# Sixteen-head attentions: the mask of the first pass moved from TensorE into VectorE's maximum

## The reference, cut to what matters

```
rel = k_off[None, :] - bs - q_off[:, None]
mask = (jnp.abs(rel) <= w) & valid            # w = bs = 128
scores = jnp.where(mask, q @ k.T * scale, -inf)
out = softmax(scores) @ v                     # then @ Wo.T (+ bo), added to x
```

## Time and profile before

| | |
|---|---|
| median of 3 runs | 3557.51 us (3554.87 to 3571.56) |
| the profiled execution: its own time | 3537.08 us |
| its span, from first to last instruction | 3535.1 us |
| TensorE matmuls busy | 2807.6 us (79%), 22894 instructions |
| VectorE busy | 1827.2 us (52%), 3518 instructions |
| ScalarE busy | 1385.0 us (39%) |
| GpSimd busy | 757.2 us (21%) |
| mean granted TensorE clock | 0.877 of full |
| units of the causal attention | 1268 to 1549 us of the span: 281.0 us |
| units of the sliding attention | 3199 to 3424 us of the span: 225.0 us |

### The profile page before, as it was taken

The page is one execution under the profiler, slowest core; times in us unless marked ns, Lnnn a source line. Parts: engine busy times, 40 slices in busy tenths (PEclk is TensorE's granted clock), DMA queues, the critical chain, the costliest instruction groups (busy, mean ns, idle before and its releaser), DMA issues. The chain is left out here.

```text
span 3535.1 us, 58022 instructions
## 1 busy us (share of the span) xinstructions
PE 2807.6 (79%) x22894; PEld 1440.1 (41%) x22894; DVE 1827.2 (52%) x3518; ACT 1385.0 (39%) x2680; POOL 757.2 (21%) x701
## 2 busy tenths in 40 slices
PE   6566877778887768889768888898887878777986
PEld 3455246523347533334322222342233433564545
DVE  5311244379874278811378888312773543626733
ACT  4210434442323337653356777422222222234551
POOL 1000006336516320000443340003530000230003
PEclk9675878978888879999979999998999989887987
DMA  2022001111101231000041010000520001022102
GB/s 110 15 64 75 0 13 40 44 61 66 66 13 41 76 69 32 22 1 0 14 71 22 11 31 1 0 0 17 132 64 0 0 1 48 17 54 66 40 5 70
DMA packets 85552, 130.19 MB, mean 37 GB/s; under 512 B 15584, under 2 KB 54464, under 8 KB 84008
## 3 DMA queue, kind: packets, MB, share of 16 engines
q1 hardware_dynamic: 73256, 108.26, 11.2%
q0 software_dynamic: 8576, 15.14, 1.8%
q10 hardware_dynamic: 3456, 3.15, 0.3%
HBM read 99.93 MB, written 25.85 MB: 36 GB/s over the span
## 5 line engine op out<-in xcount | busy, mean ns | idle before, releaser
L1758 DVE TENSOR_REDUCE at_mp<-PS 128x1 f32<-128x384 f32 (+3 forms) x640 | 306.4, 535 | 93.7 <-PE PS L1583 81.6
L1708 ACT ACTIVATE at_pt<-PS 128x384 f32<-128x384 f32 (+3 forms) x704 | 270.7, 455 | 198.5 <-PE PS L1583 165.0
L1575 PE MATMUL PS<-at_kx,at_qx 48*128 48x384 bf16 (+5 forms) x640 | 199.9, 349 | 67.5 <-PEq L77 41.0
L1603 PE MATMUL PS<-at_qx,at_kx 57*128 57x512 bf16 (+5 forms) x704 | 193.9, 315 | 9.7 <-ACT at_pt L1708 9.4
L4206 ACT ACTIVATE ls_pt<-PS,ls_far 128x512 f32<-128x512 f32 x256 | 155.3, 684 | 22.0 <-PE PS L4027 16.8
L4353 DVE CUSTOM_DVE_ANT_0 PS<-PS,ls_pt 128x1024 f32<-128x1024 f32 x128 | 153.7, 1239 | 17.8 <-ACT ls_pt L4206 15.2
L1583 PE MATMUL PS<-at_above,identb 64*128 64x128 bf16 (+1 forms) x1408 | 161.1, 212 | 0.0
L1583 PE MATMUL PS<-at_other,at_eye 64*128 64x128 bf16 (+1 forms) x1408 | 158.5, 208 | 0.0
L2478 DVE TENSOR_TENSOR_SCAN mb_ring<-PS,mb_ring 128x1024 f32<-128x1024 f32 x64 | 146.6, 2290 | 19.4 <-POOL mb_ring L2417 6.7
L2433 PE MATMUL PS<-mb_ring,ident 128*128 128x512 f32 x256 | 147.8, 730 | 6.0 <-DVE mb_ring L2483 6.0
L989 ACT ACTIVATE mx_h<-PS,small_L 128x128 f32<-128x128 f32 x312 | 88.9, 368 | 146.0 <-PE PS L873 79.2
(11 more groups left out here) (830 smaller groups left out, 6473.5 us busy)
## 6 DMA issues: line engine op xcount, KB each, us to landing
rw_arena<-rw_v_rows SPq DMA_DIRECT2D x32, 512.0 KB, 4.6
dl_arena<-in_fir_bank SPq DMA_DIRECT2D x32, 256.0 KB, 3.2
lnA<-mb_rows SPq DMA_DIRECT2D x16, 512.0 KB, 3.7
XN<-mb_rows SPq DMA_DIRECT2D x16, 512.0 KB, 3.6
ffn_place<-in_ffn_L SPq DMA_DIRECT2D x4, 1152.0 KB, 17.0
x_rows<-mx_t SPq DMA_DIRECT2D x16, 256.0 KB, 2.4
mx_s<-y_rows SPq DMA_DIRECT2D x16, 256.0 KB, 5.0
ffn_place<-in_ffn_L SPq DMA_DIRECT2D x4, 1024.0 KB, 7.9
```

Source lines behind the costliest of these rows:

```text
L1575: mm = nc.tensor.matmul(PS[:, n % 3, 0:e - c], QX[rows, u % 3, g, blk(i, P)], KX[rows, u % 3, g, c:e], start=True, stop=True)
L1603: mm = nc.tensor.matmul(PS[:, 3 + n % 3, 0:e - c], KX[rows, u % 3, g, blk(j, P)], QX[rows, u % 3, g, c:e], start=True, stop=True)
L1708: nc.scalar.activation(PT[:, y % SLOTS, g, 0:e - c], PS[:, 3 + n % 3, 0:e - c], ACT.Exp, scale=SCALE).then_inc(exp_done, 1)
L1758: nc.vector.tensor_reduce(best, sc, AX.X, ALU.max).then_inc(s_maxed, 1)
```

## The change

A table `HIDE` (128 x 512, fp32) holds +1e30 at the places that the mask hides and 0 elsewhere: in its last block for the causal attention, in its first and third for the sliding one. Where a piece of the first pass has a cut block, VectorE's instruction is `tensor_tensor_reduce` instead of `tensor_reduce`: it subtracts the fitting stretch of `HIDE` from the scores in PSUM, writes the difference back to PSUM in place, and gives the maximum. Pieces without a cut block keep `tensor_reduce`. `score_masks` goes, and the score's matmul signals `s_ready` itself. The second pass and its masks stay as they are.

```diff
+        HIDE = sb("at_hide", [P, BLK])
...
+                own(ins)
+                own(pool.memset(HIDE[:, :], 0.0))
+                for j, sign in ((3, 1),) if causal else ((0, -1), (2, 1)):
+                    ins = pool.affine_select(out=HIDE[:, blk(j, P)], in_=HIDE[:, blk(j, P)], compare_op=ALU.is_ge, fill=-NEG, base=0, pattern=[[-sign, P]], channel_multiplier=sign)
                 own(ins)
...
-                    mm = nc.tensor.matmul(PS[:, n % 3, 0:e - c], QX[...], KX[...], start=True, stop=True)
-                    if not masks_first(x):
-                        mm.then_inc(s_ready, 1)
+                    nc.tensor.matmul(PS[:, n % 3, 0:e - c], QX[...], KX[...], start=True, stop=True).then_inc(s_ready, 1)
...
-                def score_masks(u, x, t):
-                    n = N1 * u + HG * x + t
-                    i, c, e = first[x]
-                    for j in masks_first(x):
-                        mm = mask(n % 3, j * P - c, 0 if j >= i else 1, head_first(x, t) // EACH)
-                    if masks_first(x):
-                        mm.then_inc(s_ready, 1)
...
-                            for n in asked:
-                                score_masks(p, n // HG, n % HG)
...
-                        nc.vector.tensor_reduce(best, sc, AX.X, ALU.max).then_inc(s_maxed, 1)
+                        if masks_first(x):
+                            at = BLK - (e - c) if causal else c - (i - 1) * P
+                            nc.vector.tensor_tensor_reduce(sc, sc, HIDE[:, at:at + e - c], 1.0, -3e38, ALU.subtract, ALU.max, best).then_inc(s_maxed, 1)
+                        else:
+                            nc.vector.tensor_reduce(best, sc, AX.X, ALU.max).then_inc(s_maxed, 1)
```

More of the change, by code:

```diff
@@ L1574, in score @@
                     rows = lane_rows(lane, RAW)
-                    mm = nc.tensor.matmul(PS[:, n % 3, 0:e - c], QX[rows, u % 3, g, blk(i, P)], KX[rows, u % 3, g, c:e], start=True, stop=True)
-                    if not masks_first(x):
-                        mm.then_inc(s_ready, 1)
+                    nc.tensor.matmul(PS[:, n % 3, 0:e - c], QX[rows, u % 3, g, blk(i, P)], KX[rows, u % 3, g, c:e], start=True, stop=True).then_inc(s_ready, 1)
                 def mask(bank, at, kind, lane):
```

## The result

The changed kernel takes 3573.16 us (median of 18 runs, 3557.09 to 3582.31) against 3557.20 (18 runs, 3544.19 to 3576.60): ratio 1.0036, 95% interval 1.0023 to 1.0049. It is slower by some 13 us where I forecast 7 less. (Beside the experiments further down, which ran on three chips, the kernel before took 3520 to 3523 us; so kernels are compared by their ratios to it.) The profiled execution took 3581.19 us, span 3579.4, at a mean granted clock of 0.862 (before 0.877).

The account below looks back on a forecast made before the run. Second pass nearly as long as both passes together, capping gains at 31 us. Sliding -9.1, causal +0.7, steps 0 and 1 +1.0, table +0.5 sum to -6.9 us: 3557.5 to 3550.6 us, range 3537 to 3567.

Parts of the forecast that it names:

- The instruction's price: VectorE, both attentions: each tensor_tensor_reduce costs 0.03 us more than a reduce, with bounds 0 and 0.14 us.
- paid in series: Rival on VectorE: each accumulator read adds its full 0.14 us, +28 us in sum, 3585.5 us; chance 0.10.
- Its share on the path: Causal full step: about a third of the dearer maxima's 1.0 us, 0.35 us, lies where VectorE sets the pace.
- The masks' 0.25: Causal full step: VectorE's four waits for masks, 1.9 us, shorten by 0.25 us in all.
- 1.7 forecast: Causal attention: +0.7 us over 7 full steps and +1.0 us in step 0.
- The sliding gain: Sliding full steps: 0.5 + 1.1 - 0.3 = 1.3 us gained a step, 9.1 us over seven.
- I take 1.1 of the 1.54: Sliding, rounds 4 to 5: earlier-fed VectorE and an earlier turn recover 1.1 of 1.54 us lost against step 8.
- the 1.0 us wait gone: Sign in sliding full steps: TensorE's 1.0 us wait for VectorE before turning the maxima disappears, steps of 22.5 us.
- The clock, given 0.06: Rival: fewer matmuls in step 0 make TensorE's clock rise later, +1 to +14 us, 3562 us; chance 0.06.
- step 8 has fewer matmuls still and keeps 1.00: Argument against the rival of a later-rising clock: step 8, with fewer matmuls, holds granted clock 1.00.
- the counts: Both attentions: 1408 of 2816 mask matmuls go, and 512 of 640 tensor_reduce become tensor_tensor_reduce.
- The warning sign: Sliding attention: steps above 23.5 us would show the forecast wrong; full steps of 22.5 us were expected.

Follow-up runs that it names:

- e4: Kernel before, with the sliding attention's first-pass masks left out and plain tensor_reduce kept, causal attention as before; ratio 1.0003 to the kernel before.
- e7: Kernel before, all masks kept, with the turn of the maxima one round later in TensorE's queue in the sliding attention; ratio 0.9981 to the kernel before.
- e3: Changed kernel, but first-pass mask matmuls stay on TensorE with tables of zeros, beside VectorE's new instruction; ratio 1.0044 to the kernel before.
- e6: Changed kernel with the turn of the maxima one round later in TensorE's queue in the sliding attention; ratio 0.9980 to the kernel before.
- e12: Kernel before with the sliding turn of the maxima one round later and zero matmuls in step 8 of both attentions; ratio 1.0002 to the kernel before.
- e8: Changed kernel with six zero matmuls, 512 columns each, ahead of the turn of the maxima in the sliding attention; ratio 1.0018 to the kernel before.
- e10: Kernel before with only the sliding attention changed, its turn one round later, and zero matmuls in step 8 of both attentions; ratio 0.9975 to the kernel before.

## Why the prediction was wrong

**The instruction's price was too low: 0.05 us and not 0.03.** Starts at 512 keys are 0.65 us apart, each read of the accumulator beside the next one; and one stretch of eight plain reduces of the kernel before:

```profile
1293.07 0.73 DVE L1753 CUSTOM_DVE_ANT_0 PS<-PS,at_hide 128x512 f32<-128x512 f32 x1
1293.72 0.14 DVE L1753 DVE_READ_ACCUMULATOR2_ANT at_mp<- 128x1 f32 x1
1293.72 0.73 DVE L1753 CUSTOM_DVE_ANT_0 PS<-PS,at_hide 128x512 f32<-128x512 f32 x1
...
1316.87 4.87 DVE L1758 TENSOR_REDUCE at_mp<-PS 128x1 f32<-128x512 f32 x8 [0.42 <-PE PS L1575]
```

The last of the eight lasts 0.68 us, so the other seven starts lie (4.87 - 0.68) / 7 = 0.60 apart. The prediction set the new instruction's spacing (1.18 us) against a reduce's duration (1.217), but reduces too start before the one ahead has ended. The read is not paid in series. The prediction let the Trainium skill, VectorE: DVE Perf Modes, "The DRAIN you can't avoid", speak against that, but the same paragraph goes on that a next operation that is not held starts earlier. The trace agrees: the next instruction starts 0.65 us after one that lasts 0.73.

**Its share on the path was right.** I let a third of the causal step's 1.0 us count (0.35); 32 x 0.05 are 1.6 us, and a third of that is the 0.53 measured. That the share came out so close is partly luck, since it was a guess. The masks' 0.25 was 0.26. So +0.27 a step instead of +0.1, and with step 0 (first maximum to first exponential 24.80 us instead of 24.10) and the output's step, +2.4 us for 1.7 forecast. Small.

**The sliding gain was half of it: -0.65 us a step at clock 1.00, not -1.3.** The term "I take 1.1 of the 1.54" failed: 0.01 of it came. The exponentials of rounds 3 to 5 after, to be laid beside the earlier trace rows:

```profile
3342.09 1.23 ACT L1701 ACTIVATE at_pt<-PS 128x256 f32<-128x256 f32 x4 [1.18 <-PE PS L1586]
3344.08 0.96 ACT L1701 ACTIVATE at_pt<-PS 128x128 f32<-128x128 f32 x4 [0.76 <-PE PS L1586]
3347.14 0.61 ACT L1701 ACTIVATE at_pt<-PS 128x128 f32<-128x128 f32 x3 [2.11 <-PE PS L1586]
```

Round 3 to 4 went from 2.14 to 1.99 us, round 4 to 5 from 3.07 to 3.06. The turn waits for VectorE's normalise, which stands behind four maxima and a copy in VectorE's queue. Feeding VectorE earlier moved both engines by about the same amount (e4, without dearer maxima, still waits 1.0 us), and dearer maxima made the wait 1.2 us for 1.0. It was an order of two queues and not a shortage, and the one-line move of e7 took it away with all the masks in place. That my own forecast named "the 1.0 us wait gone" as a sign made this visible at once.

**The clock, given 0.06 and sought in the wrong place.** The rival had it rise later in step 1; it falls in the middle. Against the rival I wrote "step 8 has fewer matmuls still and keeps 1.00". That was the step of the argument that failed: how busy a whole step is does not decide, and step 8 doesn't always keep 1.00 either (e3, e6 and e12 in the sliding attention). The changed full step has PE busy 20.20 of 23.17 us, 87%, and steps with this work fall in four of six cases; step 8 has 17.84 of 21.27, 84%, and held. What the disturbed steps of the changed kernel have is a hole with thin work on both sides, and e8 filled the hole alone. Thin sides are not needed each time, as e3 shows. Four falls cost 25.59 + 25.14 + 28.38 + 26.93 less e8's 2 x 23.22 + 26.65 + 24.91, that is 8.0 us. By the Trainium skill, TensorE: Matmul & The Clock Gate, "A second HAM failure mode: psum-queue depth-cycling", idle moments between groups of matmuls that come often enough make the clock go back and forth; the trace agrees so far that in the step at 3284.05 the clock fell with no wait of the matmuls above 1.2 us.

**The sum.** Sliding, forecast -9.1, with +0.5 in step 0 and -0.5 in step 1; measured +2.6: full steps -3.5 at a held clock (six, with the output's), falls +8.0, steps 0 and 1 -1.1, the output -0.9. Causal +2.4, and up to 16 more where the clock falls in step 8 and the output. Outside the attentions nothing was found that follows the kernel. Of the 13 us, then, the sliding attention's +2.6 and the causal steps' +2.4 are accounted for. The rest, some 8 us, is open; falls in the causal attention, which cost up to 16 us where they came, are the candidate. GpSimd's fill took 0.53 us and a select 0.29, and the causal barrier still hides them (its wait went from 12.5 us to 11.8).

Right were the counts, the spacing of 0.61 to 0.66 us and causal steps within 0.3 us of 29.85. The warning sign that I had named, sliding steps above 23.5 us, is what came.

## What to carry to other kernels

Matmuls that a dense stretch carries "for free" also hold its clock. Before taking them out, look at 2 us windows of TensorE around its longest wait in that stretch, not at the step's mean: if the wait stands between windows that are full only because of the work to be removed, take the wait away first. That lowers the number of falls (11 of 18 full steps to 4 of 24) but does not end them. And a wait for an engine that is not short of time is cured by moving the waiting instruction in its queue, not by making either engine's work less: here that was worth 0.94 us a step alone, more than the change itself.

## What the runs showed that I had not expected

- The same instructions at the same pace lose the clock in one step and keep it in the next (1.81 and 0.81 us of PE busy in the 2 us windows ahead of the turn, in both), and the same kernel loses it in three or four steps.
- A fall costs little at once and for short: 1.7 to 2.4 us a step. Four of them outweigh 112 fewer matmuls in every full step.
- Six matmuls by a matrix of zeros in the hole were enough for 1.00 in all full steps (e8), while seven and eight of them spread over step 8 did not always help (e10 to e12).
- With all first-pass masks still streaming, but with zeros in their tables, the clock fell in two of six full steps (e3).
